# Graph attention kernel: the gathers of step g wait for the landing of step g - 1, not of step g - 2

## What is computed

```python
# layer 0: 4 heads of 32
m = x @ W_n2m.T
q, k, v = (m @ W.T + b for W, b in ((Wq, bq), (Wk, bk), (Wv, bv)))
e = (edge_attr @ W_edge.T) @ We.T
alpha = einsum(q[dst], k[src] + e) / sqrt(32)
p = exp(alpha - segment_max(alpha, dst)[dst])
out = segment_sum((v[src] + e) * p / segment_sum(p)[dst], dst)
x = layernorm(x + gate(out, m) @ W_m2n.T)
# layer 1: one head of 256
scores = sum(q1[dst] * k1[src]) / 16 + edge_weight * we + be
out = segment_sum(v1[src] * softmax_by_dst(scores), dst)
x = layernorm(x + transformer_block(x, out))
```

## Time and profile before

| what | value |
|---|---|
| median of three timed runs | 5529.07 us (5522.97 to 5533.86) |
| span of the profiled execution | 6986.8 us |
| mean granted clock of TensorE, profiled | 0.779 |
| busy: PE, DVE, POOL, ACT | 4413.6, 4304.2, 3716.2, 1729.7 us |
| gathers | 2 x 1760, of 946 and 998 ns |
| DMA queues | 1039.58 MB, mean 149 GB/s |

### The profile page before, as it was taken

How to read it: one execution, slowest core, us unless ns; L and a number is a source line. 1 busy time by engine, 2 the same in 40 slices (tenths; PEclk the granted TensorE clock), 3 DMA queues, 4 the chain that set the end, 5 groups by cost and what they waited for, 6 DMA issues and landing times.

```text
span 6986.8 us, 104716 instructions
## 1 busy us (share of the span) xinstructions
PE 4413.6 (63%) x26899; PEld 3604.4 (52%) x26899; DVE 4304.2 (62%) x14756; ACT 1729.7 (25%) x4276; POOL 3716.2 (53%) x3934
## 2 busy tenths in 40 slices
PE   5565656565555556556656666666666666666698
PEld 3455555555555555555434555444454445555577
DVE  5456655566555556556855666666665666666688
ACT  0344544444444444445210000000000000000032
POOL 1555555555555555554135555556555555555455
PEclk9677776677777677777877778888887878878899
DMA  5565655555555555554345666556666666665422
GB/s 156 150 161 156 162 158 153 152 153 159 156 152 152 153 153 158 156 160 129 110 128 149 159 157 158 157 156 159 154 163 152 154 153 160 159 159 158 123 78 71
DMA packets 777208, 1039.58 MB, mean 149 GB/s; under 512 B 206912, under 2 KB 528273, under 8 KB 776609
## 3 DMA queue, kind: packets, MB, share of 16 engines
q1 hardware_dynamic: 466736, 499.53, 28.0%
q0 software_dynamic: 169040, 436.01, 23.3%
q10 hardware_dynamic: 140832, 97.33, 4.4%
HBM read 929.76 MB, written 128.40 MB: 151 GB/s over the span
## 4 chain that ended last, share of the span: by engine, by line
DVE 31%; PE 21%; another core or an unknown queue 19%; issue 15%; DVEq 6%; DMA 3%; POOL 3%; ACT 2%; ACTq 1%; POOLq 0%; SPq 0%
PE ps L1275 19%; DVE oh L1055 4%; DVE prod L925 4%; DVE rows L902 4%; POOL rows L580 3%; DVE acc L1075 2%; DVE score L914 2%; DMA acc_d<-acc 2%; DVEq L1133 2%; DVE msg L1050 2%; DVE oht L893 2%; DVE prod L909 1%; DMA rows<-x_d,idx 1%; DVEq L339 1%
## 5 line engine op out<-in xcount | busy, mean ns | idle before, releaser
L580 POOL DMA_INDIRECT rows<-kv_d,idx x1760 | 1709.4, 971 | 1552.0 <-DVE score L914 818.6
L580 POOL DMA_INDIRECT rows<-x_d,idx x1760 | 1767.7, 1004 | 1222.5 <-DVE score L925 581.2
L1275 PE MATMUL ps<-qw,oht 128*128 128x128 bf16 (+2 forms) x12320 | 1372.0, 267 | 230.4 <-issue 199.7
L1275 PEld LDWEIGHTS ps<-qw,oht 128*128 128x128 bf16 x12320 | 1125.8, 113 | 507.7 <-issue 294.2
L1275 PE MATMUL ps<-rows,oh 128*128 128x257 f32 x3520 | 1093.1, 469 | 421.8 <-DVE oh L1055 275.0
L1275 PEld LDWEIGHTS ps<-rows,oh 128*128 128x128 f32 x3520 | 789.9, 234 | 587.9 <-DVE oh L1055 302.3
L925 DVE CUSTOM_DVE_ANT_0 prod<-rows,ps 128x256 f32<-128x256 f32 x1760 | 637.1, 418 | 653.3 <-remote 229.6
L1275 PE MATMUL ps<-msg,oh 128*128 128x132 f32 x3520 | 679.0, 348 | 507.4 <-issue 296.1
L1275 PEld LDWEIGHTS ps<-msg,oh 128*128 128x128 f32 x3520 | 582.8, 246 | 575.2 <-issue 360.0
L699 ACT ACTIVATE pen_r<-ps 128x128 f32<-128x128 f32 (+1 forms) x110 | 29.9, 272 | 3051.3 <-PE ps L1355 2249.1
L1275 PE MATMUL ps<-w_c,ea 128*128 128x128 f32 x3520 | 691.0, 350 | 146.7 <-issue 103.3
(11 more groups left out here) (201 smaller groups left out, 4423.7 us busy)
## 6 DMA issues: line engine op xcount, KB each, us to landing
dst_row<-in_dst_row SPq DMA_DIRECT2D x880, 256.0 KB
qw<-q_d SPq DMA_DIRECT2D x440, 192.8 KB
acc_d<-acc ACTq DMA_DIRECT2D x440, 128.5 KB
ea<-in_eaT SPq DMA_DIRECT2D x440, 128.0 KB
qw<-q_d SPq DMA_DIRECT2D x440, 96.0 KB
acc_d<-acc ACTq DMA_DIRECT2D x440, 66.0 KB
rows<-kv_d,idx POOLq DMA_INDIRECT x1760
rows<-x_d,idx POOLq DMA_INDIRECT x1760
```

The lines of the kernel that those rows point to most:

```text
L580: pool.indirect_dma_start(out=L.rows[par][:, st, j, 0:D], out_offset=None, in_=L.table, in_offset=bass.IndirectOffsetOnAxis(ap=idx[par][:, ...
L1275: return pe.matmul(out_, lhsT=lhsT, rhs=rhs, start=first, stop=last)
```

## The change

```diff
                         after(pool, s["msg" if L is L0 else "agg"], CH * (c - 2) + st + 1)
                         after(pool, s["score"], CH * c + st - LEAD + 1)
-                        after(pool, s["gathered"][b], 64 * n)
+                        after(pool, s["gathered"][1 - b], 64 * (n + b))
                         for j in range(JT):
                             pool.indirect_dma_start(
```

## The result

| | before | changed |
|---|---|---|
| median of four timed runs, one chip | 5526.67 us (5522.97 to 5533.86) | 8213.76 us (8200.34 to 8221.54) |
| ratio | | 1.486, 95% interval 1.485 to 1.488 |
| span of the profiled execution | 6986.8 us | 8219.8 us |

The change costs 2687 us. The forecast had the direction and the mechanism, but 7560 us and a range up to 7950 us: 654 us too little, 264 outside the range. By its length and by e15 the profiled execution before is of another chip than the timed ones.

What follows compares the result with a forecast made beforehand. GpSimd's issue was taken as the bound; issue, landing and restart sum to 7.51 and 7.74 us a step, times 440, plus 879 us for the rest, less about 25: 7564, taken as 7560 us, range 6850 to 7950.

Steps and rivals of the forecast that it cites:

- The bound: GpSimd bounds the timed runs before the change, issuing gathers almost without pause, 5.08 and 5.22 us a step.
- The two totals: Whole kernel: 5412 us with all of GpSimd's waiting taken away, against the timed median of 5529.07 us.
- Issue, 4.78 and 4.92 us: GpSimd's issue of a step's four gathers in layers 0 and 1, without the 0.30 before the first.
- Restart, 0.83 and 0.92: GpSimd, from its release to the next gather's start: 0.83 us in layer 0, 0.92 in layer 1.
- Landing, 1.9 us: From the last gather's end to the semaphore, each step: 1.5 from pauses, 0.4 for the semaphore and loads sharing engines.
- bound from above: Upper limit for the landing, read at layer 1's start with two steps and large loads in flight: 3.4 us.
- Rival B: Late landing: each takes the crowded start's 3.4 us, 8880 us in all; partly true, 8000 to 8400. Chance 0.07.
- The estimate of 7014 us: Whole kernel by the Trainium skill's DMA rule: 2.30 us from last gather's start to semaphore, 6.88 and 7.12 a step.
- The sign and the page: Slower, chance 0.96; gathers' landing ends GpSimd's idle time, not the score; profiled span within a few per cent of median.
- A: Fixed costs on GpSimd are shorter in timed runs than profiled: 5980 us if everything scales, up to 6850. Chance 0.12.
- C: The wait is hidden behind GpSimd's pauses on scores, which timed runs have too: no change, 5529 us. Chance 0.03.
- D: Faster: fewer gathers in flight on the DMA engines free ScalarE's 60.4 us of waits, 5469 us. Chance 0.02.

Runs made afterwards that it cites:

- e15: The kernel before, unchanged, run again for a profile beside its timed runs on one chip: 6985 us.
- e7: The new wait in layer 0 only, the old wait kept in layer 1, all work done: 6849 us.
- e5: The kernel before with three gathers in a step instead of four, every fourth gather left out: 4973 us, ratio 0.896.
- e14: The changed kernel with SyncE's loads and ScalarE's stores both cut to 16 partitions: 7595 us.
- e10: The changed kernel with SyncE's loads for each step cut to 16 partitions, full rows: 7805 us.
- e13: The changed kernel with ScalarE's stores of running sums cut to 16 of 128 partitions, node stages reading zero rows: 7930 us.
- e3: The changed kernel with SyncE's loads for step g + 2 also waiting until step g + 1 has landed, all work done: 7730 us.
- e11: The same edit as e3, repeated beside the changed kernel on the same chip: 7714 us, 503 under the changed kernel.
- e1: The changed kernel with SyncE's loads cut to a quarter or less in bytes, packets unchanged: 7938 us.
- e4: The changed kernel with the wait for step g - 1 between the second and third gather: 6838 us, ratio 0.967 to the kernel before.
- e12: The same edit as e4, repeated on another set: 6730 us, ratio 0.966 to the kernel before.

## Why the prediction was wrong, point by point

**The bound: right.** GpSimd issued almost without pause in the timed runs that were to be predicted. e7 shows it for layer 1, on a chip of that kind (0.44 us of mean pause), e5 supports it (573 us for three gathers instead of four). The two totals that the inference rested on, 5412 us and the median, told the truth. The prediction took the long profiled execution for stalls of that one execution; they were stalls of every run on its kind of chip.

**Issue, 4.78 and 4.92 us: right.** From a step's first gather to the end of its last it was 4.78 and 4.97. The 0.05 in layer 1 is 22 us.

**Restart, 0.83 and 0.92: right.** It was 0.86 and 0.94 in the mean, 24 us in all. The mean holds the 28 long restarts, which the prediction did not know of; a common one is 0.76 and 0.84, so part of the agreement is luck.

**Landing, 1.9 us: the step that failed.** The prediction put it: "After the change a landing step has the gather queue to itself, which is nearest to the pauses". The queue, yes; the engines behind it, no. In the pauses of the earlier trace rows the gathers landed while no load and no store moved. SyncE, whose loads follow the scores, had stood still as well; its neighbouring issues in the kernel before are

```profile
1515.87 0.00 SPq L411 DMA_DIRECT2D idx<-in_idx  x1
1525.26 0.33 SPq L430 DMA_DIRECT2D dst_row<-in_dst_row  x1
```

and the last packet of that landing came before 1524.1. In the changed kernel the loads and stores go on while GpSimd waits. Its landings were late by some 2 us at fixed places of the chunk, and took 2.56 and 2.62 us in the mean. The term was short by 0.66 and 0.72 us, times 440 each: 605 of the 654 us. Of its two parts the 0.4 to the semaphore was right (0.36 and 0.35); the 1.5 for the data was that of a clear landing, where the mean was 2.11 and 2.22. Even among the pauses of the kernel before not all were clear: over the 86 of layer 0 that last more than 4 us, the last packet ends 1.68 us after the issue in the mean, 1.49 in the median. The prediction read one of each layer. e14 gives the size in another way: 622 us between the changed kernel and the one without the neighbours' packets, 412 for the loads alone (e10), 287 for the stores alone (e13), which overlap.

**The range** ended at a landing of 2.35 us in the mean, though the prediction's own bound from above was 3.4 and the measured means lie between the two. Rival B, late landing, named the mechanism and gave 8000 to 8400 for its partial case, where the result lies; I gave it 0.07 because "no second step is in flight any more". The row from the start of layer 1 was read as two steps of gathers disturbing each other. The same moment held large loads, as the prediction itself said, and those were the part that stayed.

**The estimate of 7014 us** beside the sum, from 2.30 us between the last gather's start and the semaphore, was further off, by 1200 us. Even a clear landing is seen 2.78 us after that start (1494.81 to 1497.59), and the mean is 3.5 and 3.6. Its steps of 6.88 and 7.12 us also take the other three gathers at 3.75 and 3.90 us; put into the sum's own 4.78 and 4.92, the same 2.30 gives 6.96 and 7.14.

**The sign and the page: right.** The landing replaced the score as what ends GpSimd's waits. That the profiled span came to within 0.1% of the timed runs was forecast for a reason that did not decide it: the profiled execution after is one of the timed runs, and the kernel before shows the same agreement where both are of one chip (e15).

**Rivals A, C, D** are out by the result: 8214 is above 6850, and nothing was hidden or gained.

## What to carry to other kernels

A producer that issues transfers at the pace of the whole kernel pays for every stop for a landing, and it matters where in the step the stop stands: before the first of four gathers 2687 us here, before the last 218. When a landing moves onto the critical path, take its price from moments in which the other queues are at work, not from pauses in which no other transfer was in flight, and ask who shares its DMA engines; holding the other loads until just after a landing (e3, e11) took back 480 to 500 us. Where a profiled span is far from the timed median, look for which engine stands still without a reason, before using rows that such a stall may have made.

## What the runs showed of the hardware beyond that

- Cutting the bytes of SyncE's queue from 499.53 to 182.00 MB but none of its 466,736 packets (e1) took 276 us off; 140.59 MB in 248,496 packets (e10) took 412. How much of the difference is packets and how much the last 41 MB was not separated.
- The kernel before took 5527 to 5546 us in two sets and 6977 to 7071 in three; the changed one 8214 and 8217. A change can cost 49% on one chip and 18% on another because the time of one of its two versions goes with TensorE's idle time and that of the other does not. The timing of the kernel before on one chip alone would have hidden this.
- On chips of the second kind the wait between the second and third gather (e4, e12) *beats* the kernel before, 0.966 and 0.967. It was not run on a chip of the first kind, where the wait before the last gather loses 4%, so I don't offer it as a better version; why the later wait helps there is open.
